# A value projection in plain float32 instead of split high and low parts

## The reference

```python
# 1: attention by a running sum with rotors
v = x @ Wv.T                                   # the value projection
memory = cumsum(v * exp(1j * t * freqs), axis=1)
x = layernorm(x + real(memory * conj(rotor)) @ Wo.T)
# 2: attention over the context, scores times a decay matrix
s = (x @ ctx.T) / 16 * decay
s = s / max(|s.sum(-1)|, 1)
x = layernorm(x + s.T-weighted sum of ctx)
# 3: eight experts, the best two of each token
x = layernorm(x + mixture(x, router_w, up_proj, down_proj))
```

## Time and profile before

| | |
|---|---|
| timed runs | 270.92, 373.49 and 270.89 us; median 270.92 |
| profiled execution | span 269.3 us, the timed median lies 1.6 us above it |
| TensorE busy | 208.4 us, 77% of the span |
| VectorE busy | 169.8 us, 63% |
| GpSimd busy | 153.1 us, 57% |
| ScalarE busy | 116.8 us, 43% |
| mean granted TensorE clock | 0.915 |
| first stage | to about 110 us |

### The profile page before, as it was taken

The page is one execution under the profiler, slowest core; times in us unless marked ns, Lnnn a source line. Parts: engine busy times, 40 slices in busy tenths (PEclk is TensorE's granted clock), DMA queues, the critical chain, the costliest instruction groups (busy, mean ns, idle before and its releaser), DMA issues.

```text
span 269.3 us, 5242 instructions
## 1 busy us (share of the span) xinstructions
PE 208.4 (77%) x1393; PEld 184.8 (69%) x1394; DVE 169.8 (63%) x534; ACT 116.8 (43%) x286; POOL 153.1 (57%) x140
## 2 busy tenths in 40 slices
PE   8387698988989998857899999999999999400000
PEld 8387587977978888757688888888888888300000
DVE  5945988889889768595355455455554554207993
ACT  4352251433424420381345545454554554515665
POOL 1264857747756720085567777777777774515330
PEclk9889999999999999995999999999999999855555
DMA  7945456656543100550223223233332332079413
GB/s 222 392 163 179 136 194 223 168 176 198 205 164 119 39 22 21 189 166 2 88 79 104 86 94 99 86 97 100 97 96 87 97 95 78 12 213 318 171 78 156
DMA packets 20130, 35.75 MB, mean 133 GB/s; under 512 B 2861, under 2 KB 11312, under 8 KB 20112
## 3 DMA queue, kind: packets, MB, share of 16 engines
q1 hardware_dynamic: 16368, 26.21, 29.6%
q0 software_dynamic: 3744, 9.31, 11.3%
HBM read 27.12 MB, written 9.31 MB: 135 GB/s over the span
## 4 chain that ended last, share of the span: by engine, by line
PE 62%; DVE 17%; issue 9%; POOL 4%; DMA 4%; ACT 2%; DVEq 1%; SPq 0%; ACTq 0%; POOLq 0%
PE p_c L558 13%; PE p_v L558 7%; PE p_y L480 6%; PE p_y L584 4%; PE p_r L558 4%; PE p_a L558 4%; PE p_s L464 3%; PE p_s L558 3%; PE p_v L420 3%; PE p_t L597 3%; POOL space L1020 3%; DVE space L851 3%; PE p_r L508 2%; PE p_a L499 2%; PE p_t L446 2%
## 5 line engine op out<-in xcount | busy, mean ns | idle before, releaser
L558 PE MATMUL p_c<-w_hi,parts 128*128 x104 | 34.6, 414 | 0.0
L1044 POOL DMA_INDIRECT y_dram<-x1T,scatter_now x26 | 26.3, 1013 | 11.8 <-issue 5.3
L1024 POOL DMA_INDIRECT turns<-x_dram,gather_now x26 | 25.4, 979 | 12.6 <-issue 3.8
L823 DVE TENSOR_TENSOR parts<-p_y,parts 128x256 fp32r<-128x256 f32 x39 | 16.5, 424 | 17.6 <-ACT parts L934 17.6
L1011 POOL TENSOR_TENSOR w_lo<-keep,w_hi 128x1536 fp32r<-128x1536 f32 (+1 forms) x8 | 27.5, 3434 | 0.1
L833 DVE TENSOR_TENSOR cs<-p_c,cs 128x256 f32<-128x256 f32 x26 | 11.0, 425 | 22.6 <-ACT cs L941 22.6
L994 POOL TENSOR_TENSOR space<-back 128x512 f32<-128x512 f32 x8 | 10.2, 1271 | 18.9 <-DVE back L717 18.9
L941 ACT ACTIVATE cs<-p_c 128x256 f32<-128x256 f32 x26 | 10.1, 387 | 24.6 <-PE p_c L558 24.6
L437 PE MATMUL p_c<-const,space 128*128 128x128 f32 x128 | 17.3, 292 | 4.2 <-DVE space L671 4.2
L664 DVE TENSOR_SCALAR x<-r,mv,rs 128x256 f32<-128x256 f32 x32 | 20.2, 671 | 0.6
L1002 POOL TENSOR_TENSOR cs<-space,vinv 128x256 f32<-128x256 f32 x16 | 9.5, 612 | 18.5 <-DVE vinv L731 15.0
(11 more groups left out here) (161 smaller groups left out, 575.0 us busy)
## 6 DMA issues: line engine op xcount, KB each, us to landing
keep<-in_weights SPq DMA_DIRECT2D x8, 768.0 KB, 4.4
space<-y_dram SPq DMA_DIRECT2D x16, 256.0 KB, 4.2
space<-in_xT SPq DMA_DIRECT2D x8, 256.0 KB, 3.5
keep<-in_x SPq DMA_DIRECT2D x8, 256.0 KB, 3.5
space<-in_ctxT SPq DMA_DIRECT2D x8, 256.0 KB, 2.8
space<-in_ctxt SPq DMA_DIRECT2D x8, 256.0 KB, 3.1
x_dram<-x SPq DMA_DIRECT2D x8, 256.0 KB, 2.2
keep<-x_dram SPq DMA_DIRECT2D x1, 2048.0 KB, 8.4
```

The lines of the kernel that those rows point to most:

```text
L558: last = nc.tensor.matmul(dst, lhs[:, k, :], w[:].rearrange("p e n -> p (e n)")[:, bass.ds(start + col + k * width, width)], start=(n == 0 ...
L823: nc.vector.tensor_tensor(xs_lo[s], p_xt, xs_hi[s].bitcast(F32), ALU.subtract).then_inc(xlo_ok, 1)
L1024: nc.gpsimd.indirect_dma_start(xs[s], None, x2_dram, bass.IndirectOffsetOnAxis(ap=gather_now[s][:], axis=0)).then_inc(xs_ok[s], 16)
L1044: nc.gpsimd.indirect_dma_start(y_dram, bass.IndirectOffsetOnAxis(ap=scatter_now[s][:], axis=0), ys[s], None, bounds_check=TOPK * N - 1, oo ...
```

## The change

The value projection is a plain fp32 matmul for every pair, as it was for the first one. Per half it is 2 matmuls, where 6 were. The splits `wv_hi`, `wv_lo`, `xT_hi` and `xT_lo` are gone with their semaphores, from ScalarE (one conversion of 512 columns a pair and one for the weight) and from GpSimd (as many subtractions). TensorE now waits for the load of `xT` itself, and the load of `xT` of pair `i + 2`, into the buffer of pair `i`, waits for pair `i`'s values instead of its split. `w_hi` and `w_lo` of the experts stay. Line numbers of the changed kernel are smaller: the values are line 411, the prefix sums 427, the transposes of `x1` 436, `p_y` 467, `w_lo` 983.

```diff
@@ SP
                 if has(2):
-                    if isinstance(i, int) and i == 0:
-                        sp.wait_ge(v_ok, 1)
-                    elif has(0):
-                        sp.wait_ge(xTlo_ok, i)
+                    if has(0):
+                        sp.wait_ge(v_ok, i + 1)
                     load(xT_in, xT, xT_ok, i + 2, s)
@@ TensorE
-            def values(q, first):
+            def values(q, xT_pair):
 
-                terms = ((xT_in[0], wv),) if first else ((xT_hi, wv_hi), (xT_hi, wv_lo), (xT_lo, wv_hi))
-                for n, (xT_part, wv_part) in enumerate(terms):
-                    for k in range(KC):
-                        last = nc.tensor.matmul(p_v[:, q, :], xT_part[:, q, k, :], wv_part[:, k, :],
-                                                start=(n == k == 0), stop=(n == len(terms) - 1 and k == KC - 1))
+                for k in range(KC):
+                    last = nc.tensor.matmul(p_v[:, q, :], xT_pair[:, q, k, :], wv[:, k, :],
+                                            start=(k == 0), stop=(k == KC - 1))
                 return last
...
-                    pe.wait_ge(wvlo_ok, 1)
...
-                    first = not has(0)
-                    if first:
-                        pe.wait_ge(xT_ok[0], 16)
-                    else:
-                        pe.wait_ge(xTlo_ok, i + 1)
+                    pe.wait_ge(xT_ok[1 - s], 8 * (i + 1 - (1 - s)) + 16)
+                    if has(0):
                         pe.wait_ge(turned_ok, i + 1)
-                    values(0, first)
+                    values(0, xT_in[1 - s])
@@ ScalarE
-            act.wait_ge(wv_in, 16)
-            nc.scalar.activation(wv_hi, wv[:], ACT.Copy).then_inc(wvhi_ok, 1)
             for h in range(2):
-                if h == 1:
-                    act.wait_ge(xT_ok[1], 16)
-                    nc.scalar.activation(xT_hi, xT_in[1], ACT.Copy).then_inc(xThi_ok, 1)
...
-                if has(2) and has(0):
-                    act.wait_ge(xT_ok[s], 8 * (i - s) + 32)
-                    act.wait_ge(v_ok, i + 2)
-                    nc.scalar.activation(xT_hi, xT_in[s], ACT.Copy).then_inc(xThi_ok, 1)
@@ GpSimd
-            pool.wait_ge(wvhi_ok, 1)
-            nc.gpsimd.tensor_tensor(wv_lo, wv[:], wv_hi.bitcast(F32), ALU.subtract).then_inc(wvlo_ok, 1)
...
-                if has(2):
-                    pool.wait_ge(xThi_ok, i + 2)
-                    nc.gpsimd.tensor_tensor(xT_lo, xT_in[s], xT_hi.bitcast(F32), ALU.subtract).then_inc(xTlo_ok, 1)
```

More of the change, by code:

```diff
@@ L163, in decoder_block @@
         parts = sb("parts", [P, 4 * RING, KC, P], F32R)
-        xT_hi, xT_lo = parts[:, 0:2, :, :], parts[:, 2:4, :, :]
-        wv_hi, wv_lo = (parts[:, n:n + 2, :, :].rearrange("p a b c -> p (a b c)").rearrange("p (k d) -> p k d", k=KC)
-                        for n in (4, 6))
         shift = [sb(f"shift{s}", [P, 2]) for s in range(2)]
@@ L279, in decoder_block @@
         zeros_ok, router_in = sem("zeros_ok"), sem("router_in")
-        wvhi_ok, wvlo_ok, xThi_ok, xTlo_ok = (sem(n) for n in ("wvhi_ok", "wvlo_ok", "xThi_ok", "xTlo_ok"))
         angle_ok, sine_ok, cosine_ok, rotor_ok = (sem(n) for n in ("angle_ok", "sine_ok", "cosine_ok", "rotor_ok"))
@@ L467, in step @@
                 if has(1):
-                    values(1, first).then_inc(v_ok, 1)
+                    values(1, xT_in[1 - s]).then_inc(v_ok, 1)
                 if has(-1):
```

## The result

The changed kernel takes 262.85 us (median of 4 runs, 262.09 to 263.95), the kernel before in the same comparison 270.9. The ratio is 0.972, 95% interval 0.968 to 0.976: faster, by 8.05 us between the medians where 6.7 were forecast. The time lies 0.05 us under the lower bound of the range as it was given (262.9 to 266.5). Two later comparisons, beside other kernels, gave 263.79 and 263.11 us, ratios 0.976 (0.968 to 0.984) and 0.971 (0.966 to 0.975). Executions in the chip's slower state, about 1.5% or more above a kernel's fastest, count in the medians and not in the ratios.

A forecast was written before the change was run, and what follows sets the result against it. First-stage steps were taken as bound by TensorE, with waits for VectorE's normalisation behind GpSimd's late w_lo. Terms: 2.4 - 6.1 - 3.2 + 0.2 = -6.7 us, from 270.92 to 264.2 us; range 262.9 to 266.5.

The forecast's parts named there:

- The wait for VectorE: TensorE's waits before the x1 transposes, put down to late w_lo on GpSimd, shrink: 6.1 us saved.
- The condition on `w_hi`: In the steps, w_hi on ScalarE ends near 71.3, before cs at 71.65, so w_lo can follow cs.
- TensorE is next in line, with no gap: Prefix sums run straight into the x1 transposes in steps 3 to 6; 1.0 us of wait stays in step 2.
- The matmul term: Values in steps 1 to 6: two plain fp32 matmuls per half cost 0.41 us more per pair, +2.44 us.
- The start: Before the first p_y: turn at 8.1 saves 1.85 us, the kept clock 1.34; together -3.2 us.
- The 0.2 us for wait instructions: On TensorE, one more wait instruction per step in four steps, between transposes and values; at most 0.6 us, 0.2 allowed.
- The forecast's own interval: End time if the forecast holds: 264.2 us, within 263.2 to 265.2, given 69%.
- The clock rival: At the start TensorE's clock is still lost after 2.4 us idle, 1.34 us stay: 265.5 us; 20% including its variant.
- Its variant: At the start a late clock rise stretches pair 0's values to near 9.0, 0.9 us lost: 265.1 us; within the 20%.
- The two rivals in which the gap stays, by half or whole: Gap before the x1 transposes: closes by half only, 267.2 us, 6%; or stays, not GpSimd's doing, 272.0 us, 2%.
- The slower rival: Expert weights land just in time for w_hi, so the steps gain nothing and matmuls cost more: 273.3 us; 3%.

The follow-up runs named there:

- e2: Kernel before with six fp32r matmuls kept, all pairs reading pair 1's split, so the steps' xT splits are gone: 263.81 us, ratio 0.972.
- e4: Changed kernel with a GpSimd subtraction of the removed one's size, result unread, put ahead of w_lo: 270.7 us, ratio 0.998.
- e5: Changed kernel with a ScalarE conversion of 512 columns, result unread, put ahead of w_hi: 265.24 us, ratio 0.979.
- e1: Kernel before with plain fp32 matmuls for every pair's values, splits kept and waited for but unread: 271.93 us, ratio 1.005.
- e3: Changed kernel with the start's conversions and subtractions of wv and xT 1 put back, unread: 264.41 us, ratio 0.971.
- e6: As e2, with two fp32r matmuls per half instead of six, leaving out part of the values' work: 265.49 us, ratio 0.980.
- e6b: As e2, with four fp32r matmuls per half instead of six, leaving out part of the values' work: 265.44 us, ratio 0.979.
- e9: As e2, with ten fp32r matmuls per half instead of six, so work is added: 266.97 us, ratio 0.984.
- e7: Kernel before with 16 filler matmuls ahead of the first prefix sums: 270.61 us against 271.68, ratio 0.998.

## Why the prediction was right, and where it was off

- **The wait for VectorE was GpSimd's doing, and goes.** Right, with its size: 6.1 us forecast, 6.01 in the trace. e2 has it alone, e4 takes it back. The condition on `w_hi`, that it ends near 71.3 and so before `cs` does, was real: with ScalarE's part left in (e5) 0.3 us a step stay.
- **TensorE is next in line, with no gap.** Right in steps 3 to 6; 1.0 us stayed in step 2, as worked out.
- **The matmul term was mis-sized.** "Six pairs, in steps 1 to 6, remain on a busy TensorE: +2.44 us" measured +0.37 (changed kernel) and +0.47 (e1). The change of the matmuls alone is the 0.47: against e2, which keeps the six, the changed kernel has 0.50 more over the six distances, and the missing 0.1 comes with the splits' going, by a way that no run shows. I took a TensorE whose instructions follow each other closely for one that is bound by its own work. `x1T` and `att` are made in time that the values fill, and about 0.87 us of each half are free. A half was also 0.87 us and not the 0.915 of `p_y`, and so nearly fits. The estimate from the Trainium skill, "FP8 and Floating Point Precision", section "TensorE Precision Notes" (0.95 us a half), was further off: 0.87 is 3.7 times the pace of the fp32r matmuls per column, not 4.
- **The start.** VectorE's stretch, `turn` at 8.1 and the clock kept: right in the profiled run. 2.83 instead of 3.2, because `back` waited for the last rotor, which my sum never asked about. But I took the start of before from one profile, and it was a bad one. In the seven profiles with the start's splits and without fillers (before, e1, e2, e3, e6, e6b, e9) `turn` starts at 9.08 to 10.07 and the first `p_y` at 15.56 to 17.38; only before and e6b have two stretched instructions, and e9 kept the clock. The changed kernel's three have `turn` at 8.08 to 8.12 and `p_y` at 14.53 to 14.97. The gain is 0.6 to 2.9 us, 1.9 between the means. e4 and e5, which lack these splits too, came to 15.44 and 15.96, with the constants landing late.
- **The 0.2 us for wait instructions** didn't appear as a term of its own; whatever there is of it is inside the +0.37.
- **The sum** came out 1.4 us short of the median's gain: the matmuls +2.1 and the wait instruction +0.2 too dear, the start 0.4 and the gaps 0.1 too good, which makes 8.5 in the profile, and 8.05 over the runs. That the time falls on the range's bound, and not further under it, owes something to luck: the matmuls' error and those of the start and the gaps have opposite signs. The forecast's own interval, 263.2 to 265.2, was missed.
- **The rivals.** The clock rival did happen, in one of three profiles of the changed kernel. It cost 0.42 us there, not 1.34. Its variant didn't: the values of pair 0 took 1.89 us from 5.21 and were done before `turn` at 8.12. The two rivals in which the gap stays, by half or whole, fall with the traces. The slower rival didn't come about: with free queues `w_lo` followed `cs` at once in every step. That weights landing late could have done it was not tried.

Open are what decides which idle time costs the clock, and how much of the start's gain the timed runs hold: the runs of e3, which takes it back, show nothing clear of noise.

## What to carry to other kernels

A dense row of matmuls is not yet a bound: ask of each group what the instruction after it waits for, since work that lies in another engine's round trip is free up to the length of that trip, and making it cheaper gains nothing. An operation of GpSimd costs what VectorE's instruction behind it loses, so look at what ends when it ends; here a subtraction of 1.27 us a step that nobody on TensorE waited for, with the conversion that fed it, was worth 6 us in five steps. Price a change to the start of a kernel with a spread, from several profiles of the kernel before, because what meets what there depends on when transfers land.

## What the runs showed of the hardware that I had not expected

Idle time alone doesn't tell whether TensorE's clock falls. It stayed at 2.4 GHz after 2.44 us (changed) and 2.49 us (e4) at the start, and fell to 1.2 GHz after 2.59 us (e3) and 2.75 us (the changed kernel again). Yet in e9 it stayed after 2.93 us:

```profile
10.56 2.02 PE L439 MATMUL p_c<-const,space 128*128 128x128 f32 x16 [2.93 <-DVE space L674]
```

In step 2, 2.17 us cost nothing in the kernel before, and about the same cost the clock in e4 and e7.

GpSimd's subtraction held up VectorE's instructions of one form and not of another. A scalar_tensor_tensor of two SBUF operands and the tensor_scalar took 1.24 to 1.38 us beside it instead of 0.29 to 0.42. Additions with one operand in PSUM were not held up, before:

```profile
71.60 0.69 DVE L746 TENSOR_TENSOR r<-p_y,keep 128x512 f32<-128x512 f32 x1
...
73.46 0.69 DVE L707 TENSOR_TENSOR r<-p_a,x 128x512 f32<-128x512 f32 x1
```

The first ran beside the `xT_lo` subtraction, the second beside `w_lo`; at 104.31, with neither, the second's form took 0.68 us. The Trainium skill, "SBUF — State Buffer", section "Who interferes with whom", says that a VectorE instruction with two SBUF inputs contends with a GpSimd instruction that reads SBUF, that tensor_scalar can use the pair of ports that VectorE shares with GpSimd, and that in that mode whoever issues first keeps the pair for its whole instruction. The traces agree: the held instructions ended 0.15 to 0.29 us after GpSimd's.
